# A fused attention and feed-forward block on one Trainium2 core: the order of work inside the slots of a software pipeline, with some lags changed

## What is computed

```python
q = _ln(fp8_linear(ln_out, wq), qln_w, qln_b)          # per head of 128
k = _ln(fp8_linear(ln_out, wk), kln_w, kln_b)
v = fp8_linear(ln_out, wv)
core = softmax(q @ k.T * 128**-0.5) @ v                # per head, 8 groups g of 2 heads
xout = the same with qx, and kx, vx from the context
cat = concatenate([core, xout])
out = einsum(fp8(clip(cat / smooth)), wproj) * scale
x = x + out
x = x + down(silu(gate(layernorm(x))) * up(layernorm(x)))
```

## Time and profile before

| what | value |
|---|---|
| median of 3 runs | 2232.85 us (2229.85 to 2239.35) |
| profiled execution, its own time | 2232.37 us |
| its span | 2230.6 us |
| mean granted TensorE clock | 0.967 |
| first and last scores matmul (L647) | 206.4 and 1839.4 us |
| TensorE busy | 1758.1 us, 79% |
| VectorE, ScalarE, GpSimd busy | 68%, 63%, 52% |

### The profile page before, as it was taken

One profiled execution on the slowest core, in us unless ns is written; L12 is line 12 of the kernel. 1 busy time (PEld: TensorE's weight loads), 2 busy tenths in 40 slices (PEclk: granted clock), 3 DMA queues, 4 the chain that ended last, 5 costly groups with the idle time before them and its releaser, 6 DMA issues.

```text
span 2230.6 us, 48222 instructions
## 1 busy us (share of the span) xinstructions
PE 1758.1 (79%) x15776; PEld 1242.5 (56%) x15776; DVE 1517.2 (68%) x3480; ACT 1416.1 (63%) x2926; POOL 1165.2 (52%) x1045
## 2 busy tenths in 40 slices
PE   0126888888887888788888878887888857999998
PEld 0024666666666666666666656666666633444443
DVE  8994887777678768877776787688777744233332
ACT  2335877877777778777767777777788854221311
POOL 3554656665665666666656656665666640211202
PEclk9997999999999999999999999999999978999999
DMA  4001656665676666666656765675567698020200
GB/s 146 28 29 24 120 105 114 130 124 96 116 117 120 107 113 130 110 112 126 128 96 103 126 118 105 118 129 105 103 138 150 128 260 268 13 113 10 103 19 19
DMA packets 639383, 240.88 MB, mean 108 GB/s; under 512 B 612496, under 2 KB 612496, under 8 KB 638608
## 3 DMA queue, kind: packets, MB, share of 16 engines
q1 hardware_dynamic: 639120, 237.62, 52.7%
HBM read 65.57 MB, written 20.97 MB: 39 GB/s over the span
## 4 chain that ended last, share of the span: by engine, by line
issue 39%; POOL 25%; PE 13%; DVE 10%; ACT 8%; SPq 1%; DMA 1%; POOLq 1%; ACTq 0%; DVEq 0%
POOL local L975 15%; POOL local L960 4%; PE ps_pj L565 4%; ACT local L766 4%; DVE neg_max L1194 3%; POOL head_rstd L953 3%; POOL local L991 2%; PE ps_qt L584 2%; ACT local L787 2%; ACT local L841 2%; DVE local L1094 1%; PE ps_s L649 1%; PE ps_o L633 1%; PE ps_s L647 1%; PE ps_o L635 1%
## 5 line engine op out<-in xcount | busy, mean ns | idle before, releaser
L975 POOL TENSOR_TENSOR local<-local 128x512 bf16<-128x512 f32 x512 | 601.8, 1175 | 186.4 <-ACT local L841 186.2
L565 PE MATMUL ps_pj<-wide 128*128 (+2 forms) x5544 | 603.4, 258 | 52.2 <-ACT local L766 39.5
L838 ACT ACTIVATE local<-ps_s,neg_max 128x512 f32<-128x512 f32 x512 | 359.0, 701 | 371.7 <-DVE neg_max L1194 366.7
L565 PEld LDWEIGHTS ps_pj<-wide 128*128 128x128 bf16 x5544 | 476.1, 100 | 190.1 <-issue 45.8
L953 POOL TENSOR_TENSOR head_rstd<-head_var,minus_half 128x3 f32<-128x3 f32 x256 | 218.2, 852 | 459.8 <-DVE head_var L1161 459.8
L1194 DVE TENSOR_REDUCE neg_max<-ps_s 128x1 f32<-128x512 f32 x512 | 349.4, 682 | 158.2 <-PE ps_s L649 157.3
L633 PE MATMUL ps_o<-v_hi,local 128*128 128x129 bf16 x2048 | 388.7, 226 | 37.0 <-DMA local<-local 22.3
L635 PE MATMUL ps_o<-v_hi,local 128*128 128x129 bf16 x2048 | 388.1, 223 | 0.0
L634 PE MATMUL ps_o<-local 128*128 128x128 bf16 x2048 | 387.8, 222 | 0.0
L841 ACT ACTIVATE local<-ps_s,neg_max 128x512 bf16<-128x512 f32 x512 | 357.5, 698 | 12.6 <-DMA local<-local 12.6
L584 PE MATMUL ps_qt<-ident,local 128*128 128x128 f32 x768 | 131.3, 296 | 213.7 <-ACT local L787 167.3
(11 more groups left out here) (111 smaller groups left out, 2866.4 us busy)
## 6 DMA issues: line engine op xcount, KB each, us to landing
w_raw<-w_group SPq DMA_DIRECT2D x32, 512.0 KB, 4.3
quantised_heads<-local SPq DMA_DIRECT2D x32, 512.0 KB, 3.1
wide<-quantised_heads SPq DMA_DIRECT2D x4, 4096.0 KB, 13.8
local<-local SPq DMA_TRANSPOSE x640, 3.2
local<-x SPq DMA_DIRECT2D x4, 1024.0 KB, 5.6
local<-ctx_t SPq DMA_DIRECT2D x4, 1024.0 KB, 4.8
w_raw<-w_proj SPq DMA_DIRECT2D x8, 512.0 KB, 4.0
wide<-w_proj SPq DMA_DIRECT2D x4, 1024.0 KB, 6.0
```

What stands on the lines that cost most here:

```text
L565: last = mm(dst[:, at:at + n], lhs, w_at(par, part, c, cross * 512 + at, n), start=(k == 0), stop=(k == len(terms) - 1))
L838: a(p_exp[:, u % 2], ps_s[u % 2][:], ACT.Exp, bias=neg_max[:, u % 4:u % 4 + 1])
L975: tt_(pp[:, u % PP_BUFS, 1], p_exp[:, u % 2], pp[:, u % PP_BUFS, 0], ALU.subtract)\
```

## The change

No instruction is added or removed in the 64 slots of a group. In each engine's slot the pieces stand in another order, and some lags differ: `FULL_LAG` 1 to 0, `Y_LAG` 6 to 5, `QUANT_LAG` 6 to 7, `SUMS_LAG` 3 to 4, `W_HI_LAG` 9 to 10, and on SyncE `TURN_LAG`, `HEAD_LAG`, `STORE_LAG` each one more. `turn_at` is written differently and gives the same slots. The order in a slot becomes:

- TensorE: PV, (in the last group the early matmuls of the projection), turn, project, scores. Before: turn, project, early matmuls, PV, scores.
- ScalarE: (last group: convert), squares and v_part, qk_high, head_norm, exponentials, weight_hi, qk_whole. Before: squares and v_part, weight_hi, exponentials, head_norm, qk_high, qk_whole of the slot before.
- VectorE: weight_sums, maximum, second part of quantising, reciprocal, tile work, first part of quantising, weight_scale, weight_lo, y. Before: weight_sums, reciprocal, maximum, y, both parts of quantising, tile work, weight_scale, weight_lo.
- GpSimd: qk_rest, the difference, head_power. Before qk_rest was last.

With `STORE_LAG` the last group has 16 slots of tail, before 15.

```diff
@@ -296,14 +296,14 @@
-        MAX_LAG, EXP_LAG, LO_LAG, TURN_LAG = 1, 1, 2, 3
-        PV_LAG, Y_LAG, HEAD_LAG, STORE_LAG = 5, 6, 9, 11
+        MAX_LAG, EXP_LAG, LO_LAG, TURN_LAG = 1, 1, 2, 4
+        PV_LAG, Y_LAG, HEAD_LAG, STORE_LAG = 5, 5, 10, 12
         SQ_LAG, VAR_LAG, QN_LAG = 1, 1, 2
-        QT_FIRST, QT_STEP = 10, 2
-        QK_LAG, FULL_LAG, REST_LAG = 0, 1, 3
-        QUANT_LAG, QUANT_END_LAG = 6, 8
+        QT_SLOTS = (10, 12, 14)
+        QK_LAG, FULL_LAG, REST_LAG = 0, 0, 3
+        QUANT_LAG, QUANT_END_LAG = 7, 8
         PREP_FIRST, PREP_STEP = 4, 10
-        SUMS_LAG, SCALE_LAG, SCALE_PIECES, W_HI_LAG, W_LO_LAG = 3, 5, 2, 9, 11
+        SUMS_LAG, SCALE_LAG, SCALE_PIECES, W_HI_LAG, W_LO_LAG = 4, 5, 2, 10, 11
         SMOOTH_SLOT, RSMOOTH_SLOT = 22, 31
         UNIT_FREE = PV_LAG
...
-            step, odd = divmod(slot - lag - QT_FIRST, QT_STEP)
-            q, j = divmod(step, TT)
             n = GROUP_TILES // TT - (2 if last else 0)
-            return [(q, j)] if not odd and j < 3 and q < n and (q >= 0 or not first) else []
+            at = [divmod(slot - lag - first_slot, 2 * TT) for first_slot in QT_SLOTS]
+            return [(q, j) for j, (q, rest) in enumerate(at) if rest == 0 and q < n and (q >= 0 or not first)]
...
                 for slot in slots(last):
-                    for q, j in turn_at(slot, 0, first, last):
-                        turn_qk(q, j, GROUP_TURNS * g + 3 * (2 + q) + j, GROUP_TILES * g + TT * (3 + q))
-                    k, half = slot // 2, slot % 2
-                    if k < (GROUP_TILES - TILES if last else GROUP_TILES):
-                        project((b + 1) % B, i, half, (g + 1) % 2 if b == B - 1 else g % 2, GROUP_TILES * g + TILES + k)
...
                     for u in unit_at(slot, PV_LAG, first):
                         b, cross = u // UNITS, u // TT % HEADS // HPG
...
                         last_mm.then_inc(pv_done, 1)
...
+                    for q, j in turn_at(slot, 0, first, last):
+                        turn_qk(q, j, GROUP_TURNS * g + 3 * (2 + q) + j, GROUP_TILES * g + TT * (3 + q))
+                    k, half = slot // 2, slot % 2
+                    if k < (GROUP_TILES - TILES if last else GROUP_TILES):
+                        project((b + 1) % B, i, half, (g + 1) % 2 if b == B - 1 else g % 2, GROUP_TILES * g + TILES + k)
                     for u in unit_at(slot, 0, first):
                         b, head, qt = u // UNITS, u // TT % HEADS, u % TT
                         cross, hh = head // HPG, head % HPG
...
             def group(g, first, last):
                 for slot in slots(last):
...
                     for k in tile_at(slot, SQ_LAG, first, last):
                         b, i = tile_place(k)
...
                         v_part(b, i, t)
-                    for c in prep_at(slot, W_HI_LAG, last):
-                        weight_hi((g + 1) % 2, c, CH * g + CH + c + 1)
+                    for q, j in turn_at(slot, QK_LAG, first, last):
+                        qk_high(q, j, GROUP_TURNS * g + 3 * (2 + q) + j)
+                    for k in tile_at(slot, QN_LAG, first, last):
+                        head_norm(tile_place(k)[1], GROUP_TILES * g + TILES + k, GROUP_TURNS * g + 3 * (1 + k // TT))
                     for u in unit_at(slot, EXP_LAG, first):
                         act.wait_ge(max_done, SLOTS * g + u + 1)
                         if not first or u >= 2:
...
                         a(pp[:, u % PP_BUFS, 0], ps_s[u % 2][:], ACT.Exp, bias=neg_max[:, u % 4:u % 4 + 1])\
                             .then_inc(exp_done, 1)
-                    for k in tile_at(slot, QN_LAG, first, last):
-                        head_norm(tile_place(k)[1], GROUP_TILES * g + TILES + k, GROUP_TURNS * g + 3 * (1 + k // TT))
-                    for q, j in turn_at(slot, QK_LAG, first, last):
-                        qk_high(q, j, GROUP_TURNS * g + 3 * (2 + q) + j)
-                    for q, j in turn_at(slot, FULL_LAG, first, last):
-                        qk_whole(q, j, GROUP_TURNS * g + 3 * (2 + q) + j)
...
+                    for c in prep_at(slot, W_HI_LAG, last):
+                        weight_hi((g + 1) % 2, c, CH * g + CH + c + 1)
+                    for q, j in turn_at(slot, FULL_LAG, first, last):
+                        qk_whole(q, j, GROUP_TURNS * g + 3 * (2 + q) + j)
...
                 for slot in slots(last):
+                    for q, j in turn_at(slot, REST_LAG, first, last):
+                        qk_rest(q, j, GROUP_TURNS * g + 3 * (2 + q) + j)
                     for u in unit_at(slot, LO_LAG, first):
                         pool.wait_ge(exp_done, SLOTS * g + u + 1)
...
                     for k in tile_at(slot, VAR_LAG, first, last):
                         head_power(tile_place(k)[1], GROUP_TILES * g + TILES + k)
-                    for q, j in turn_at(slot, REST_LAG, first, last):
-                        qk_rest(q, j, GROUP_TURNS * g + 3 * (2 + q) + j)
...
                 for slot in slots(last):
                     for c in prep_at(slot, SUMS_LAG, last):
                         weight_sums(c, CH * g + CH + c + 1)
-                    for u in unit_at(slot, Y_LAG, first):
-                        dve.wait_ge(pv_done, SLOTS * g + u + 1)
-                        v.reciprocal(r_sum[:, u % 4:u % 4 + 1], ps_o[u % 2][:, D:D + 1]).then_inc(rsum_done, 1)
                     for u in unit_at(slot, MAX_LAG, first):
                         dve.wait_ge(s_done, SLOTS * g + u + 1)
                         v.tensor_reduce(neg_max[:, u % 4:u % 4 + 1], ps_s[u % 2][:], AX_X, ALU.max, negate=True)\
                             .then_inc(max_done, 1)
+                    for H in head_at(slot, QUANT_END_LAG, first):
+                        dve.wait_ge(total_done, GROUP_HEADS * g + H + 1)
...
+                        v.scalar_tensor_tensor(heads_n[:, H % 2], ps_y[:], -KEEP4, summed, ALU.mult, ALU.add)\
+                            .then_inc(heads_done, 1)
+                    for u in unit_at(slot, Y_LAG, first):
+                        dve.wait_ge(pv_done, SLOTS * g + u + 1)
+                        v.reciprocal(r_sum[:, u % 4:u % 4 + 1], ps_o[u % 2][:, D:D + 1]).then_inc(rsum_done, 1)
+                    for k in tile_at(slot, VAR_LAG, first, last):
+                        head_variance(tile_place(k)[1], GROUP_TILES * g + TILES + k)
+                    for H in head_at(slot, QUANT_LAG, first):
+                        dve.wait_ge(y_done, SLOTS * g + TT * (H + 1) + UNIT_FREE)
...
+                    for piece in range(SCALE_PIECES):
+                        for c in prep_at(slot, SCALE_LAG + 2 * piece, last):
+                            weight_scale(c, piece, CH * g + CH + c + 1)
+                    for c in prep_at(slot, W_LO_LAG, last):
+                        weight_lo((g + 1) % 2, c, CH * g + CH + c + 1)
                     for u in unit_at(slot, Y_LAG, first):
                         H, qt = u // TT, u % TT
                         dve.wait_ge(rsum_done, SLOTS * g + u + 1)
...
                             .then_inc(y_done, 1)
-                    for H in head_at(slot, QUANT_LAG, first):
-                        dve.wait_ge(y_done, SLOTS * g + TT * (H + 1) + UNIT_FREE)
...
-                    for H in head_at(slot, QUANT_END_LAG, first):
-                        dve.wait_ge(total_done, GROUP_HEADS * g + H + 1)
...
-                    for k in tile_at(slot, VAR_LAG, first, last):
...
-                        head_variance(tile_place(k)[1], GROUP_TILES * g + TILES + k)
-                    for piece in range(SCALE_PIECES):
-                        for c in prep_at(slot, SCALE_LAG + 2 * piece, last):
-                            weight_scale(c, piece, CH * g + CH + c + 1)
-                    for c in prep_at(slot, W_LO_LAG, last):
-                        weight_lo((g + 1) % 2, c, CH * g + CH + c + 1)
```

56 lines of the change are left out of this document (27 added, 29 removed).

## The result

The changed kernel takes 2057.64 us in the median of 4 runs (2050.22 to 2060.29), against 2233.73 us before: a ratio of 0.9205, 95% interval 0.9172 to 0.9238. The forecast was 2018 us with a range of 1955 to 2110, so the direction and the size class were right and the gain was 40 us smaller than forecast. The profiled execution took 2050.22 us.

What follows compares the result with a forecast made beforehand. Bound: a loop of waits from turn to turn through ScalarE's `qk_whole`, 6.38 us per two slots. 160.3 + 7.2 + 9 = 176.5 us a group saves 197 us in seven groups, 18 in the last: 2232.4 - 215 = 2018 us (1955 to 2110).

Steps and rivals of the forecast that it cites:

- The bound and the cut: TensorE's turns wait for ScalarE's `qk_whole`; moving it ahead a slot cuts that loop, freeing up to 26 us a group.
- No new loop through `qk_high`: Exponentials now wait for the turn through `qk_high`, but 0.9 to 1.3 us of room remains before TensorE's scores.
- VectorE's lumps: VectorE's work in four weight preparations exceeds TensorE's by 11.2 us; less 4 of room, 7.2 us a group of waiting.
- The clock: TensorE's clock in the groups, at an unchanged 0.97, would cost 5 us of 160.
- slot costs: TensorE's own time without waits: 2.20, 2.70, 2.23 or 2.64 us a slot by kind, 160.3 us a group.
- Borders and late landings: Waits at group borders and for DMA transposes that land late: 4 us a group.
- normally in time, by 1.6 us: Transposes before PV, now first in TensorE's slot: ready after 10.1 us, needed after 11.7 us.
- The sum: Seven groups at 176.5 in place of 204.6 us, the last at 184 in place of 202: 215 us less, 2018 us.
- Half the gain: Rival: three nearly equally busy engines pay for each other's late hand-overs; 190 us a group, 2125 us, chance 0.22.
- The slower rival: TensorE's PV waits for its transpose and sets the pace; 215 us a group, 2316 us, chance 0.05.
- The port rule: VectorE's `weight_scale` and GpSimd lock each other out of a shared port; a faster pace adds 2.7 us a group.
- the 21 us: Extra time over the forecast if VectorE's collisions with GpSimd grow with the pace, at 2.7 us a group.

Runs made afterwards that it cites:

- the edit that made the old kernel 15% slower: Kernel before with only VectorE's order and lags of the changed kernel (`Y_LAG` 5, `QUANT_LAG` 7): 2568.66 us, ratio 1.1498.
- the best one: Kernel before with ScalarE's order of the changed kernel alone, and VectorE's long reciprocal moved from slot 31 to slot 55: 2015.24 us, ratio 0.9018.

## Why the prediction was right, and where it was off

**The bound and the cut.** Right, and shown from both sides: the idle time before the turns is 0.0 after, ScalarE's order alone gives the gain, and undoing ScalarE alone loses 111 us of it.

**No new loop through `qk_high`.** Right: ScalarE's pair and TensorE's pair both take 4.9 us and TensorE does not wait for the turn's bank. ScalarE's pair was worked out as 4.9.

**VectorE's lumps, 7.2 us a group.** Right in size. The waits they can cause, for y 18.5 us and for exponentials 21.5 us in six groups, are 6.7 us a group. The split between lumps and other causes is argued from the releasers, not separated by a run. The worst place was slot 33, as forecast, and one instruction makes it: the long reciprocal of slot 31 runs from 468.31 for 3.34 us, the maximum behind it starts at 471.57, its exponentials at 472.23, and the scores at 473.56 have waited 3.02 us. In part the size is luck: VectorE's own work in these slots did not stay as it was (the port rule, below).

**The clock: a term that was too large.** 5 us were taken. TensorE's busy time is 992.6 / 6 = 165.4 us a group, 5.1 over the 160.3 worked out from slot costs, and that looks like the 5. But the clock was 0.99, which makes under 2 us of 165. Some 3 more, by estimate, is time lost in waiting that counts as busy: a scores matmul is recorded as 0.38 us long where the next one starts after 0.22, so 0.16 us of a wait behind it is hidden, and some 19 slots a group waited. That the 5 came out right was luck.

**Borders and late landings: the term that was mis-sized.** I took 4 us a group. Measured are 45.9 + 9.6 us in six groups, 9.3 a group. The step "normally in time, by 1.6 us" failed as a mean that says nothing of the slots: with PV first in TensorE's slot, a transpose that is late by more than that is paid, before it had turn and project to hide behind. How much of it GpSimd's and SyncE's new order adds is not shown. A part is at the group's border. SyncE's timeline there in the whole change:

```profile
914.58 1.23 SPq L458 DMA_TRANSPOSE local<-local  x1
919.11 0.37 SPq L447 DMA_DIRECT2D w_raw<-w_group  x1
919.84 3.88 SPq L458 DMA_TRANSPOSE local<-local  x2
923.93 1.79 SPq L466 DMA_TRANSPOSE local<-local  x1
926.04 1.27 SPq L458 DMA_TRANSPOSE local<-local  x1
```

For 3.3 us SyncE issues nothing, though GpSimd's difference for the next transpose is done at 916.5; then a weight load goes ahead of the late transposes. That the loop's turning is what holds SyncE is taken from the place and not shown. PV of slot 1 waits 1.71 us for one of them. The two border slots hold 3.2 us of these waits a group.

**The sum.** Forecast 160.3 + 7.2 + 9 = 176.5 us a group; measured 160.3 + 6.7 + 9.3 + 5.1 = 181.4, and 181.9 by the window, the rest being small waits. The first group was shorter, so the first seven took 1264 / 7 = 180.6 us each, 28 us over the forecast in all. The last group was forecast at 184 in place of 202 and took 188; its DMA share was 0.91. Start and end changed nothing: from the first to the last scores matmul the kernel took 1633 us before and 1451 after, and what lies around that is 599 us in both. That is the 32 us between 2018 and the profiled 2050.

**The rivals.** Half the gain (2125) did not come, though part of its cause did, as late hand-overs at PV. The slower rival, PV waiting for its transpose, was the right place and a fifth of its size (7.7 us of waits for transposes a group against 215 - 176.5 = 38.5): landings stayed at 3.3 us in the median with the DMA share at 0.74. What I had not seen as a rival is that the parts of the change work against each other: TensorE's and VectorE's new orders together cost 24 us, on top of some 6 or 7 for GpSimd's and SyncE's.

**The port rule.** The Trainium skill (SBUF — State Buffer, "Who interferes with whom") says that whichever of VectorE in a two-port mode and GpSimd starts first holds the shared pair for its whole instruction. The prediction had such collisions grow with the pace, and this case's traces agree: they did. GpSimd's share of a group rose to 71% (127.95 of 180.6). The median of `weight_scale` hides it, 343 ns against 341, since most of the instructions meet nothing. Its mean rose from 540 to 714 ns. Over the groups, before and then after (L1208 and L1207 are the first quantising step):

```profile
L1043 DVE TENSOR_SCALAR w_raw<-w_raw,w_mean,wscale 128x128 f32<-128x128 f32 x196 | 94.4, 540 | 0.0
L1208 DVE TENSOR_SCALAR local<-local 128x512 int16<-128x512 int16 x126 | 80.9, 642 | 4.3
```

```profile
L1042 DVE TENSOR_SCALAR w_raw<-w_raw,w_mean,wscale 128x128 f32<-128x128 f32 x196 | 128.6, 714 | 0.0
L1207 DVE TENSOR_SCALAR local<-local 128x512 int16<-128x512 int16 x126 | 36.3, 288 | 0.0
```

The timeline after shows one such stretch. Four instructions of `weight_scale`, which took 1.11 us together at 909.25 us of the kernel before, with hardly any GpSimd work beside them, take 3.82 here beside two kinds of GpSimd instruction (L959 `qk_rest`, L976 the difference) that follow each other without a gap:

```profile
822.88 3.82 DVE L1042 TENSOR_SCALAR w_raw<-w_raw,w_mean,wscale 128x128 f32<-128x128 f32 x4
822.93 1.16 POOL L959 TENSOR_TENSOR local<-local 128x512 bf16<-128x512 f32 x1
824.05 2.32 POOL L976 TENSOR_TENSOR local<-local 128x512 bf16<-128x512 f32 x2
```

In both kernels no `weight_scale` instruction without a GpSimd instruction beside it took over 344 ns, and those with one rose from 91 to 136 of 196. So `weight_scale` costs 34 us more, 4.9 a group with weight preparation, where 2.7 were worked out. VectorE's busy time of a group fell all the same, from 158.1 to 155.8 us, because the first quantising step became 45 us cheaper in its new place in the slot. How much of the kernel's time the 34 us make is not shown. The 2.7 us a group also hold for seven groups, not eight, so the 21 us would be 19.

## What to carry to other kernels

When every engine is under 85% busy, follow the chain from one instruction of the bound engine to its next and look for the resource that closes it; here it was one PSUM bank whose last reader stood one pair of exponentials too late. Cut that by moving the reader, and change nothing else until it is measured: one engine's order gave 9.2%, and the rest of the change took 1.2 points back. In a static schedule a lag and a place in the slot are one decision across two engines. `Y_LAG` 5 with PV late in TensorE's slot cost 56 us, shown by that one number. It was also in the edit that made the old kernel 15% slower. And compare means or sums, not medians, when only some instructions of a kind are disturbed.

## What was not expected of the hardware

The granted clock changed with the same matmuls. Over the middle groups it was 0.91 at 248 us a group, 0.97 before, 0.99 in the whole change and 1.00 in the best one. It did not follow the sum of the waits: with ScalarE's order alone TensorE was idle less than in the whole change, 12 us a group against 16, and the clock was 0.98. In the six middle groups of the whole change it stood at the lower of its two levels in six short stretches. Each of them came on behind one of the longest waits, that of slot 33 or that of slot 1. Behind the 3.02 us before the scores of slot 33 at 473.56, for instance:

```profile
474.80:478.20 3.40, 3.40 (x19) 2.47 (x17) 2.24 (x7) 3.40 (x9) 3.29 (x4) 0.50 0.11 23
```

With the long reciprocal moved away, the wait of slot 33 and the low clock behind it are both gone. DMA transposes landed in 3.3 us in the median at a DMA share of 0.74 as at 0.65 (3.2 us). In the last group, at a share of 0.91, it was 3.9 us in the whole change and 3.4 with ScalarE's order alone: the share by itself says little about the latency there.
